# A graph network's attention edges: SyncE's store program as a loop with registers, or written out

## The chip, the cores and the metric

The kernel runs on one core of a Trainium2 chip. What counts is the device time of one execution in microseconds (us). Engines are named as the profile names them: PE is TensorE, DVE is VectorE, ACT is ScalarE, POOL is GpSimd, SP is SyncE. SyncE computes nothing here; it waits for semaphores and issues transfers.

## What is computed

Two graph layers over 12,500 nodes and 200,000 edges, with edges sorted by their destination `dst`. The first layer is a convolution over edges, the second is a pair of attention layers (GAT, four heads of 64 features). The change lies in the attention layers, which the reference writes as:

```python
feat = (h @ W).reshape(n, H, F)
el = jnp.sum(feat * al[None], axis=-1)
er = jnp.sum(feat * ar[None], axis=-1)
e = jax.nn.leaky_relu(el[src] + er[dst], NEG_SLOPE)
m = jax.ops.segment_max(e, dst, num_segments=n)
ex = jnp.exp(e - m[dst])
denom = jax.ops.segment_sum(ex, dst, num_segments=n)
a = ex / denom[dst]
msg = feat[src] * a[:, :, None]
out = jax.ops.segment_sum(msg, dst, num_segments=n)
```

So for each edge a row of `feat` is fetched by `src`, weighted, and the rows of one destination are added up.

## The kernel before

`gat_edges` does the edge part of one attention layer; it runs twice (two stages, with a stage of node work between them). Each of the 128 partitions walks through its own run of 1563 consecutive edges. The run is cut into `SB` = 49 segments of `SBT` = 32 edges. A segment lives in one of `B` = 3 buffers, `gb[:, p]`, with p = s % 3. Five engines work side by side, each with a program of its own, and they meet only at semaphores:

- GpSimd (`rows`, L1821) fetches a segment: 32 indirect transfers, one for each edge place, each of 128 rows. Before a segment `free` waits for three things: the indices `ix` are there (`s_ix`), the stores out of this buffer have landed (`s_st`, segment s-3), and VectorE has finished the first four rows of segment s-2 (`s_sum.at(s, 1, back=2)`).
- VectorE (`body`) starts a segment with L1893 to L1905 (scores, running maximum), waits for ScalarE's exponentials, and then runs a chain of 32 dependent row additions L1927. For each four rows there is one weighting L1915, made one group ahead. The weighting of group k+1 also raises `s_sum`, which tells that group k-1 is done.
- ScalarE makes the exponentials (L1854) and copies the denominators into the rows (L1857).
- SyncE (`body`, L1781 to L1790) stores the finished rows: for each group of four rows a wait for `s_sum` (L1789) and one transfer (L1790) to `sums`; eight of them a segment. Before them it waits until the segment's gathers have landed (L1784), loads the indices of segment s+3 into the same buffer's `ix` (L1779), and waits for ScalarE's copies (`s_seg`, L1788).

On each of these engines the first 45 segments run in a hardware loop `Fori` of 15 rounds, three segments in a round (`LOOPS` = 15). The counter's register gives SyncE the place of a store in DRAM and the values that its waits compare with. What is left is written out behind the loop: segments 45 and 46 in the same `body` with plain numbers, and the last two segments in halves (`ENDS`, function `end`, L1792 to L1796). In `body` a `nop(nofuse=True)` keeps the wait apart from the transfer; in `end` there is none.

PE has no work in these stages.

Of the kernel before, what the change touches and what calls it, by code (L numbers as in the profile page):

```python
# [18 lines left out]
SBT = 32  # L19
SB = -(-E // (SBT * P))  # L20
# [42 lines left out]
def bc(ap, dim, shape):  # L63
    return ap.unsqueeze(dim).to_broadcast(shape)
# [1662 lines left out]
def gat_edges(nc, q, n):  # L1727
# [9 lines left out]
    NQ, B, W = SBT // 4, 3, SBT + 1  # L1737
    LOOPS = (SB - 2) // B
    SPAN = 224
    SPANS = -(-CE // SPAN)  # L1740
    with ExitStack() as c:
# [3 lines left out]
        gb = sb(c, f"gb_g{n}", [P, B, SBT, GR])  # L1745
# [3 lines left out]
        wv = [pb(c, f"wv{k}_{n}", [P, 4, D]) for k in range(2)]  # L1749
        same = sb(c, f"same_g{n}", [P, SBT])  # L1750
        end_masks = [[sb(c, f"end_{y}{x}_{n}", [P, H * (t1 - t0 + 1)], BF16) for y in ("add", "back", "mul")] for x, (_, t0, t1) in enumerate(ENDS)]
        acc = sb(c, f"acc_g{n}", [P, D])

# [3 lines left out]
        s_g = [Signal(q.sem(nm(f"g{p}")), per=SBT, inc=16) for p in range(B)]  # L1757
# [6 lines left out]
        s_st = [Signal(q.sem(nm(f"st{p}")), per=NQ, inc=16, ahead=1) for p in range(B)]  # L1764
        s_dv = q.sem(nm("dv"))
        s_mask = q.sem(nm("mask"))
        out_v = q.sums1.rearrange("(p e) c -> p e c", p=P)
        quads = lambda t0, t1: [slice(t, min(t + 4, t1)) for t in range(t0, t1, 4)]
        summed = lambda x: s_sum.at(SB - 2, 0) + sum(len(quads(t0, t1)) for _, t0, t1 in ENDS[:x])
        line = lambda y, m: y[:, :, :].rearrange("p h t -> p (h t)")[:, 0:H * (m + 1)]  # L1770
        heads = lambda y, m: line(y, m).rearrange("p (h t) -> p h t", h=H)
# [3 lines left out]
        with nc.Block(no_gpsimd_drain=True) as block:  # L1775
            @block.sync
            def _(eng):
                def indices(s, p):
                    eng.dma_start(ix[:, p, :], a["src_chunks"].rearrange("p (s t) -> s p t", t=SBT)[s, :, :]).then_inc(s_ix[p].sem, 16)  # L1779

                def body(s, i, p, more):  # L1781
                    if more:
                        eng.wait_ge(s_g[p].sem, s_g[p].at(i))
                        eng.nop(nofuse=True)  # L1784
                        indices(i * B + (p + B), p)
                    eng.wait_ge(s_seg.sem, s_seg.at(s))
                    for k, ts in enumerate(quads(0, SBT)):
                        eng.wait_ge(s_sum.sem, s_sum.at(s, k + 1))  # L1788
                        eng.nop(nofuse=True)  # L1789
                        eng.dma_start(out_v[:, bass.ds(s * SBT + 4 * k, 4), :], gb[:, p, ts, :]).then_inc(s_st[p].sem, 16)  # L1790

                def end(x, s, t0, t1):  # L1792
                    eng.wait_ge(s_seg.sem, s_seg.at(SB - 2 + x))
                    for k, ts in enumerate(quads(t0, t1)):
                        eng.wait_ge(s_sum.sem, summed(x) + k + 1)
                        eng.dma_start(out_v[:, s * SBT + ts.start:s * SBT + ts.stop, :], gb[:, s % B, ts, :]).then_inc(s_st[s % B].sem, 16)  # L1796

                for s in s_st:
                    eng.sem_inc(s.sem, s.base)
                for p in range(B):  # L1800
                    indices(p, p)
                eng.dma_start(ch, q.er_start[0:EC, :].rearrange("(p e) h -> p (e h)", p=P)).then_inc(s_ch, 16)
                eng.dma_start(q.sums1_x[EC:, 0:D], a[f"L1_gnn_b{n}"].unsqueeze(0).to_broadcast([EP + 1 - EC, D])).then_inc(s_none, 16)
                eng.dma_start(q.sums1_x[EC:EP, D:GR].rearrange("(p r) c -> p r c", p=P), bc(q.unit[:, :], 1, [P, (EP - EC) // P, GR - D])).then_inc(s_none, 16)
                eng.dma_start(q.sums1_x[EP:, D:GR], q.unit[0:1, :]).then_inc(s_none, 16)
                with eng.Fori(0, LOOPS) as i:
                    for p in range(B):
                        body(i * B + p, i, p, True)
                for p in range(B - 1):
                    body(LOOPS * B + p, LOOPS, p, p == 0)  # L1810
                for x, e in enumerate(ENDS):
                    end(x, *e)
                eng.wait_ge(s_st[0].sem, s_st[0].at(SB // B, sum(len(quads(t0, t1)) for s, t0, t1 in ENDS if s == SB - 1)))
                for p in range(1, B):
                    eng.wait_ge(s_st[p].sem, s_st[p].at(SB // B - 1))
                eng.wait_ge(s_none, 48)
# [197 lines left out]
```

## Time and profile before

| what | value |
|---|---|
| time, median of 3 runs | 8455.34 us (8423.16 to 8462.91) |
| the profiled execution's span | 8387.7 us |
| GpSimd busy | 5479.5 us, 65% of the span |
| VectorE busy | 5313.3 us, 63% of the span |
| GpSimd's gathers in the edge stages, L1821 | 3126, 2962.1 us busy, 1567.2 us idle before them |
| VectorE's row additions, L1927 | 3024, 1448.4 us busy, 1278.1 us idle before them |
| SyncE's stores of the edge stages, `sums<-gb_g` | 780 transfers of 528.0 KB, and 2 of 396.0 KB |

The profiled execution is one of its own; its span, from the first to the last instruction, is 67.6 us shorter than the median of the runs. Times within the profile are counted from the start of the span. "Idle before" is the time in which the engine did nothing just ahead of such instructions; it costs something only where the engine is the one that others wait for. In the profile SyncE's instructions are listed as SPq: EVENT_SEMAPHORE is a wait, FUSED_REGOPS, MOVE and ALU_OP work on registers, DMA_DIRECT2D issues a transfer.

### The profile page before, as it was taken

To read this page: it belongs to the slowest core of one execution; us is meant where nothing else is said; L and a number is where in the kernel's file an instruction comes from. 1 tells how busy PE (TensorE), PEld (TensorE's weight loads), DVE (VectorE), ACT (ScalarE), POOL (GpSimd) and SP (SyncE) were. 2 spreads that over 40 slices of the span, in tenths; PEclk is the share of its full clock that TensorE was granted. 3 is DMA by queue.
4 is the path that set the end of the run, shared out by engine and by line. 5 is a ranking of instruction groups with operands and counts; after the bars stand their busy time and mean duration, and the time that the engine had idled before them with its cause. 6 is when DMAs were issued, how large, how long until landed. Compare 5 with 4: busy or idle time off the path is not lost. (4 is left out here: it accounts for less than half of the span.)

```text
span 8387.7 us, 62428 instructions
## 1 busy us (share of the span) xinstructions
PE 2475.3 (30%) x11337; PEld 1696.4 (20%) x11337; DVE 5313.3 (63%) x9727; ACT 2244.0 (27%) x5114; POOL 5479.5 (65%) x5324
## 2 busy tenths in 40 slices
PE   5777677777777485000000000014000000000000
PEld 4444444444444264000000000003000000000000
DVE  6777788877777476465555555653355555565556
ACT  3666677766766352000000000002000000000002
POOL 4777677776777446666666666646666666666664
PEclk8888889988988698555555555557555555555555
DMA  7555555555555457565655555643555555555566
GB/s 236 160 162 163 155 170 169 171 164 160 169 168 164 121 151 204 172 192 184 189 179 187 181 186 181 189 153 93 151 186 185 181 184 184 186 185 187 182 191 219
DMA packets 791709, 1466.03 MB, mean 175 GB/s; under 512 B 188921, under 2 KB 522174, under 8 KB 791100
## 3 DMA queue, kind: packets, MB, share of 16 engines
q0 software_dynamic: 250192, 671.13, 29.9%
q1 hardware_dynamic: 541420, 793.88, 27.1%
q8 instruction: 28, 0.46, 0.0%
q14 instruction: 69, 0.57, 0.0%
HBM read 752.61 MB, written 713.36 MB: 175 GB/s over the span
## 5 line engine op out<-in xcount | busy, mean ns | idle before, releaser
L1821 POOL DMA_INDIRECT gb_g<-table,ix_g x3126 | 2962.1, 948 | 1567.2 <-issue 937.9
L585 POOL DMA_INDIRECT gb<-table,src x1563 | 1890.5, 1210 | 698.2 <-issue 472.9
L1927 DVE SCALAR_TENSOR_TENSOR gb_g<-gb_g,same_g,wv 128x256 f32<-128x256 f32 x3024 | 1448.4, 479 | 1278.1 <-DVE gb_g L1927 554.9
L1096 PE MATMUL pm<-ident,tl 128*4 128x128 f32 x2 | 0.7, 374 | 4655.1 <-DMA tl<-sums 4655.1
L619 PE MATMUL po<-parts,sel 128*128 128x256 f32 x3930 | 1034.6, 414 | 530.7 <-ACT ost L685 347.6
L1854 ACT ACTIVATE ww<-ee 128x132 f32<-128x132 f32 (+3 forms) x102 | 28.5, 280 | 4157.9 <-DVE ee L1905 2160.6
L1915 DVE TENSOR_TENSOR wv<-gb_g,ww 128x1024 f32<-128x1024 f32 x782 | 954.7, 1221 | 0.0
L1096 PEld LDWEIGHTS pm<-ident,tl 128*4 128x4 f32 x2 | 0.2, 81 | 4656.0 <-DMA tl<-sums 4656.0
L619 PEld LDWEIGHTS po<-parts,sel 128*128 128x128 f32 x3930 | 769.5, 204 | 778.4 <-issue 543.4
L762 DVE TENSOR_TENSOR pt<-gb,pt 128x256 f32<-128x256 f32 x392 | 164.6, 420 | 584.5 <-ACT pt L679 451.2
L679 ACT ACTIVATE pt<-pt,sh 128x128 f32<-128x128 f32 x1568 | 436.9, 345 | 344.4 <-remote 200.2
L666 ACT ACTIVATE sq<-iota_f,behind 128x128 f32<-128x128 f32 x1568 | 503.3, 413 | 0.0
L609 PE MATMUL pt<-m,r 64*128 64x256 f32 x3136 | 453.2, 407 | 122.3 <-DVE parts L774 96.8
L685 ACT ACTIVATE ost<-po 128x1024 f32<-128x1024 f32 x393 | 403.2, 1026 | 320.7 <-remote 226.7
L602 PE MATMUL pm<-r,m 128*128 128x512 f32 x784 | 387.7, 618 | 43.6 <-ACT r L661 25.8
L742 DVE TENSOR_TENSOR dots<-gb,sh 128x768 f32<-128x768 f32 x392 | 370.6, 945 | 33.4 <-DMA gb<-table,src 29.7
L729 DVE TENSOR_TENSOR parts<-parts 128x768 f32<-128x768 f32 x393 | 373.7, 951 | 0.0
L766 DVE TENSOR_TENSOR parts<-pt,sh 128x768 f32<-128x768 f32 x392 | 371.3, 947 | 0.0
L769 DVE TENSOR_TENSOR parts<-gb,pt 128x768 f32<-128x768 f32 x392 | 369.9, 944 | 0.0
L609 PEld LDWEIGHTS pt<-m,r 64*128 64x128 f32 x3136 | 285.0, 189 | 401.2 <-issue 386.4
L661 ACT ACTIVATE r<-pm 128x1024 f32<-128x1024 f32 x294 | 301.6, 1026 | 200.1 <-remote 94.0
L774 DVE TENSOR_TENSOR parts<-gb,pt 128x512 f32<-128x512 f32 x392 | 265.2, 677 | 0.0
(302 smaller groups left out, 4182.0 us busy)
## 6 DMA issues: line engine op xcount, KB each, us to landing
sums<-gb_g SPq DMA_DIRECT2D x780, 528.0 KB
sums<-ost SPq DMA_DIRECT2D x393, 512.0 KB
gb_g<-table,ix_g POOLq DMA_INDIRECT x3126
gb<-table,src POOLq DMA_INDIRECT x1563
table<-f SPq DMA_DIRECT2D x48, 520.0 KB
x<-in_x SPq DMA_DIRECT2D x50, 256.0 KB
at<-in_rbf SPq DMA_DIRECT2D x100, 128.0 KB
hT_d<-hT SPq DMA_DIRECT2D x49, 256.0 KB
```

The costliest lines, as they stand in the source:

```text
L585: eng.indirect_dma_start(out=gb[:, group(k), half(k) + j, 0:4, :].rearrange("p a c -> p (a c)"), out_offset=None, in_=q.table0[:, :], in_o ...
L602: ins = eng.matmul(pm[:, g, :], m23[:, n, :], r[n][:, g, :], start=True, stop=True)
L609: ins = eng.matmul(pt[k % 2][:, 2 * h + j, :], r3[hid(h), pair(k), group(k) % 2, j0:j0 + P], m4[hid(h), :], start=True, stop=True)
L619: ins = eng.matmul(po[:, j, :], sel[:, k % 4, j, :], y.rearrange("p a c -> p (a c)"), start=y is parted[0], stop=y is parted[-1])
L666: ins = eng.activation(sq[:, 4 * (k % 2) + j, :], q.iota_f[:, :], ACT.Square, scale=2.0, bias=behind2[:, bass.ds(i * (4 * K) + (4 * (k - 1 ...
L679: ins = eng.activation(w, w, ACT.Copy, scale=sh[:, group(k), 4 * ((k - 1) % 2) + j, 0:1])
L685: eng.activation(ost[:, k % 4, :, :], po[:, :, :], ACT.Copy).then_inc(s_ev.sem, 1)
L729: eng.tensor_tensor(m, m, tmp[:, k % 4, 0:BOTH, :, :], ALU.add).then_inc(s_msg.sem, 1)
L766: eng.tensor_tensor(msg[:, b, :, 1:4, :], bc(w[:, :, 1, :], 2, [P, 4, 3, C]), s1, ALU.mult)
L1821: eng.indirect_dma_start(out=gb[:, p, j, 0:FR], out_offset=None, in_=q.table1[:, :], in_offset=bass.IndirectOffsetOnAxis(ap=ix[:, p, j:j + ...
L1915: return eng.tensor_tensor(wv[k % 2][:, 0:n, :].rearrange("p t (h c) -> p t h c", c=C), f, bc(w, 3, [P, n, H, C]), ALU.mult)
L1927: ins = eng.scalar_tensor_tensor(rows[:, t0 + t, 0:D], row, same[:, t:t + 1], wv[k % 2][:, j, :], ALU.mult, ALU.add)
```

## The change

SyncE's loop in `gat_edges` is replaced by straight code: all 47 whole segments are written out by the Python program, so that each store has its place and each wait its value as a constant. The `nop(nofuse=True)` in front of the transfers is gone, so that a wait may become part of the transfer behind it. The programs of the other four engines keep their loops; number, size and order of the transfers and what each waits for stay as they were. It is made for both attention layers.

```diff
--- before.py
+++ after.py
@@ -1778,16 +1778,14 @@
                 def indices(s, p):
                     eng.dma_start(ix[:, p, :], a["src_chunks"].rearrange("p (s t) -> s p t", t=SBT)[s, :, :]).then_inc(s_ix[p].sem, 16)
 
-                def body(s, i, p, more):
+                def body(s, p, more):
                     if more:
-                        eng.wait_ge(s_g[p].sem, s_g[p].at(i))
-                        eng.nop(nofuse=True)
-                        indices(i * B + (p + B), p)
+                        eng.wait_ge(s_g[p].sem, s_g[p].at(s // B))
+                        indices(s + B, p)
                     eng.wait_ge(s_seg.sem, s_seg.at(s))
                     for k, ts in enumerate(quads(0, SBT)):
                         eng.wait_ge(s_sum.sem, s_sum.at(s, k + 1))
-                        eng.nop(nofuse=True)
-                        eng.dma_start(out_v[:, bass.ds(s * SBT + 4 * k, 4), :], gb[:, p, ts, :]).then_inc(s_st[p].sem, 16)
+                        eng.dma_start(out_v[:, s * SBT + 4 * k:s * SBT + 4 * k + 4, :], gb[:, p, ts, :]).then_inc(s_st[p].sem, 16)
 
                 def end(x, s, t0, t1):
                     eng.wait_ge(s_seg.sem, s_seg.at(SB - 2 + x))
@@ -1803,11 +1801,8 @@
                 eng.dma_start(q.sums1_x[EC:, 0:D], a[f"L1_gnn_b{n}"].unsqueeze(0).to_broadcast([EP + 1 - EC, D])).then_inc(s_none, 16)
                 eng.dma_start(q.sums1_x[EC:EP, D:GR].rearrange("(p r) c -> p r c", p=P), bc(q.unit[:, :], 1, [P, (EP - EC) // P, GR - D])).then_inc(s_none, 16)
                 eng.dma_start(q.sums1_x[EP:, D:GR], q.unit[0:1, :]).then_inc(s_none, 16)
-                with eng.Fori(0, LOOPS) as i:
-                    for p in range(B):
-                        body(i * B + p, i, p, True)
-                for p in range(B - 1):
-                    body(LOOPS * B + p, LOOPS, p, p == 0)
+                for s in range(SB - 2):
+                    body(s, s % B, s + B < SB)
                 for x, e in enumerate(ENDS):
                     end(x, *e)
                 eng.wait_ge(s_st[0].sem, s_st[0].at(SB // B, sum(len(quads(t0, t1)) for s, t0, t1 in ENDS if s == SB - 1)))
```

## Rows read from the trace of the kernel before

**Rows 1.** Windows of the two edge stages: us, busy PE, PEld, DVE, ACT, POOL; clock, DMA.

```profile
3301.00:5594.00 2293.00, 0.00 (x0) 0.00 (x0) 1322.00 (x2480) 61.58 (x167) 1466.80 (x1550) 0.50 0.58 183
5901.00:8225.00 2324.00, 0.00 (x0) 0.00 (x0) 1334.09 (x2524) 43.59 (x153) 1482.86 (x1565) 0.50 0.58 183
```

**Rows 2.** GpSimd's gathers L1821 in the first stage: xcount, min/median/max ns; then idle, times.

```profile
L1821 POOL DMA_INDIRECT gb_g<-table,ix_g x1344: 940/946/1097, 3463.8 to 5405.6; - x192
...
  issue: 402.7, 1322
  DVE wv L1915: 221.1, 17
  DMA sums<-gb_g: 67.4, 5
```

**Rows 3.** VectorE's weighting L1915 in two stretches: first and last start.

```profile
L1915 DVE TENSOR_TENSOR wv<-gb_g,ww x6: 1220/1222/1222, 5045.6 to 5060.9; 128x1024 f32<-128x1024 f32 x6
...
L1915 DVE TENSOR_TENSOR wv<-gb_g,ww x4: 1220/1220/1222, 5085.7 to 5106.7; 128x1024 f32<-128x1024 f32 x4
```

**Rows 4.** SyncE's store line L1790 in two stretches, then over both stages.

```profile
L1790 SPq DMA_DIRECT2D sums<-gb_g x5: 332/333/710, 5050.1 to 5062.4; - x5
...
L1790 SPq DMA_DIRECT2D sums<-gb_g x5: 691/700/709, 5084.6 to 5112.6; - x5
...
L1790 SPq MOVE sums<-gb_g x720: 2/691/1397, 3337.4 to 8085.4; - x180
```

**Rows 5.** GpSimd's timeline, restarts: start, duration, instruction [idle before <-what ended it].

```profile
5047.53 0.94 POOL L1821 DMA_INDIRECT gb_g<-table,ix_g  x1 [13.21 <-DVE wv L1915]
...
5140.55 0.94 POOL L1821 DMA_INDIRECT gb_g<-table,ix_g  x1 [13.05 <-DVE wv L1915]
...
5419.90 0.94 POOL L1821 DMA_INDIRECT gb_g<-table,ix_g  x1 [13.35 <-DVE wv L1915]
...
6179.39 0.94 POOL L1821 DMA_INDIRECT gb_g<-table,ix_g  x1 [13.51 <-DMA sums<-gb_g]
...
6320.83 0.95 POOL L1821 DMA_INDIRECT gb_g<-table,ix_g  x1 [19.70 <-DVE wv L1915]
...
8093.33 0.94 POOL L1821 DMA_INDIRECT gb_g<-table,ix_g  x1 [12.84 <-DVE wv L1915]
```

**Rows 6.** VectorE's timeline, first holes after a restart, in the same columns.

```profile
5076.92 0.48 DVE L1927 SCALAR_TENSOR_TENSOR gb_g<-gb_g,same_g,wv 128x256 f32<-128x256 f32 x1 [0.92 <-DVE gb_g L1927]
...
6221.53 0.48 DVE L1927 SCALAR_TENSOR_TENSOR gb_g<-gb_g,same_g,wv 128x256 f32<-128x256 f32 x1 [0.92 <-DVE gb_g L1927]
...
8139.13 0.48 DVE L1927 SCALAR_TENSOR_TENSOR gb_g<-gb_g,same_g,wv 128x256 f32<-128x256 f32 x1 [0.48 <-DVE gb_g L1927]
```

**Rows 7.** SyncE's stores with constant places, and its loops' branch.

```profile
L1796 SPq DMA_DIRECT2D sums<-gb_g x30: 332/332/432, 5538.8 to 8219.0; - x30
...
L1806 SPq COMPARE_BRANCH  x30: 2/700/712, 3493.8 to 8089.6; - x30
```

**Rows 8.** Written-out ends of both stages: SyncE's waits and stores; VectorE's weighting L1915.

```profile
L1789 SPq EVENT_SEMAPHORE  x15: 17/17/3968, 8090.3 to 8141.9; - x15
...
L1790 SPq DMA_DIRECT2D sums<-gb_g x15: 332/332/394, 8092.6 to 8142.0; - x15
...
L1790 SPq DMA_DIRECT2D sums<-gb_g x6: 332/332/700, 5455.5 to 5491.0; - x6
...
L1915 DVE TENSOR_TENSOR wv<-gb_g,ww x4: 1219/1222/1223, 5457.4 to 5478.4; 128x1024 f32<-128x1024 f32 x4
```

**Rows 9.** VectorE's timeline, a segment's start-up from L1893 to the second L1915, twice.

```profile
5065.96 0.18 DVE L1893 COPY same_g<-samep 128x32 f32 x1 [0.28 <-DVE gb_g L1927]
...
5071.33 1.22 DVE L1915 TENSOR_TENSOR wv<-gb_g,ww 128x1024 f32<-128x1024 f32 x1
...
5119.86 0.18 DVE L1893 COPY same_g<-samep 128x32 f32 x1 [1.79 <-remote]
...
5134.42 1.22 DVE L1915 TENSOR_TENSOR wv<-gb_g,ww 128x1024 f32<-128x1024 f32 x1
```

## The prediction

> **What bounds the kernel now.** First the windows of the two attention edge stages: 2293.0 and 2324.0 us, 4617 of the span's 8387.7 us [rows 1]. The diff touches nothing outside them, so the rest of the kernel is left alone.
>
> Next GpSimd's gathers, since neither it nor VectorE is busy all the time. In the first stage 1344 gathers, 42 segments of 32, run from 3463.8 us to the restart at 5419.90 us: 1956.1 us, 46.57 us a segment. One gather takes 0.946 us and 402.7 / 1322 = 0.305 us lie before the next [rows 2, 5], so an unbroken stream would need 32 x 1.251 = 40.0 us. The other 6.6 us are pauses: 221.1 us in 17 that VectorE's L1915 ends and 67.4 us in 5 that a store's landing ends. GpSimd may gather segment s only when the first four rows of s-2 are summed, so a pause says that VectorE is late.
>
> Why it is late is in the weighting L1915, one for each four rows. In one stretch six stand from 5045.6 to 5060.9 us, 3.06 us apart; in another four stand from 5085.7 to 5106.7 us, 7.0 us apart. One takes 1.22 us in both, so VectorE isn't computing longer, it stands idle [rows 3]. With its start-up of 5.4 or 14.6 us [rows 9] and eight such steps, a segment takes some 30 to 34 us at the quick pace and 70 us at the slow one. GpSimd needs 40.0: only slow stretches cost time.
>
> SyncE has the same two paces. Quick: a transfer holds it for 333 ns. Slow: 700 ns, and the transfers of five stores stand from 5084.6 to 5112.6 us, 7.0 us apart, which is five instructions (wait, two for the place, transfer, counter) at 1.4 us. A register move, which has less to do than a transfer, has a median of 691 ns over the loops: SyncE is in the slow pace for more than half of them [rows 4].
>
> When does it turn? A gather stream restarts at 5047.53 us; VectorE shows its first 0.92 us hole at 5076.92, 29 us later; the next restart is 5140.55, so a cycle of two segments is 93.02 us, 46.5 each. The other kind restarts at 6179.39, has its first hole before 6221.53, 42 us later, and restarts at 6320.83: 141.44 us, three segments ((141.44 - 19.70) / 1.251 = 97, that is 96 gathers and a small rest), 47.1 each [rows 5, 6]. So turning 13 us later was worth nothing: the cycle holds one segment more, and all of its third segment is slow. Of the first layer's 42 segments and 22 pauses, 18 cycles of two and 2 of three make both counts.
>
> **The change part by part.** *What goes.* In the loop a segment costs SyncE 8 stores x 5 instructions and some 6 for the indices and the segment's wait; after it, one transfer that carries its wait, for each store, one more wait for a segment's first store, and one transfer for the indices: about 45 instructions become 10. The kernel has such stores already: 30 at L1796, 332 ns each [rows 7]. Directly this is worth 8 x 4 instructions of an estimated 30 ns (the quick wait is 17 ns [rows 8]), about 1 us a segment of SyncE's time at the quick pace. It lies beside VectorE's 34 to 70 us and takes nothing off the path: a store's landing ended 5 pauses of 22, and the first rows of the next segment follow it by little. Without that cover the most would be those 67.4 us of pauses in each stage.
>
> *The loop's branch* goes too, 30 of them, median 700 ns like any other SyncE instruction and at most 712 [rows 7]; 30 x 0.7 = 21 us of SyncE, hidden in the same way. The Trainium skill ("Runtime: NRT & Kernel Launch", Instruction fetch mechanics) says that a taken branch can cost a fetch of its target while straight code is streamed. By it the unrolling would gain at each branch; the row shows no branch longer than its neighbours, so I count none. About a thousand instructions of straight code more for both layers are fetched; none of the straight stores that exist shows a hole, so that is nothing as well.
>
> *What it may do to the slow stretches* is the only term of size. The kernel of before ends each stage with straight SyncE code of two instructions a store (the loop is over, the rest is written out), which is a trial of half the change. In the second layer the stream restarts at 8093.33 us. From 8092 to 8142 SyncE makes 15 stores, waits at 17 ns median and transfers between 332 and 394 ns: it doesn't turn slow at all. VectorE has its first hole before 8139.13, 46 us after the restart [rows 5, 6, 8]. In the loop SyncE was slow 33 us after a restart [rows 4, 5]. So a light SyncE moves the turn from 29 us, or 42, to about 46. But it doesn't abolish it, and once slow it changes nothing: in the first layer's end SyncE's transfers are at 332 ns and VectorE's L1915 still stands 7.0 us apart, 5457.4 to 5478.4 [rows 8].
>
> What 46 us gives: all cycles become those of three segments. Against 141.44 us the turn is 4 us later; VectorE gains 4 x (1 - 3.06 / 7.0) = 2.3 us, so 139.1 us, 46.4 a segment. If the turn comes still later, past the second segment's end, the third one's start-up runs quick: 5065.96 to 5071.33 is 5.4 us, the slow one 5119.86 to 5134.42 is 14.6 us [rows 9]. That takes off 9.2 us more, 129.9 us, 43.3 a segment. One instruction a store is lighter than the two of the trial, so I go a little past the first value, by its row the nearer: 46.0. Against 46.57 that is 0.57 us on some 94 segments (two layers of 49, less the written-out ends): 54 us.
>
> The bounds: no slow stretch at all, 40.0 us a segment, 94 x 6.6 = 620 us less. On the other side all cycles as the worst seen, 47.1: 94 x 0.55 = 52 us more.
>
> The profiled execution has 8387.7 us of span, the median of the runs is 67.6 us above it; what lies around the span isn't changed. 8387.7 - 54 = 8334, and with those 67.6, 8401 us.
>
> **The rivals.** (a) *Later turn*, as above: 8401 us, 8300 to 8430. For it: no slow SyncE instruction in 49 us of the trial [rows 8]. Against it: one trial, in which VectorE's code was straight too from 8111 us on.
>
> (b) *Nothing*: the turn isn't SyncE's doing, and SyncE is only a second victim of what slows VectorE. For it: with SyncE idle between its stores VectorE stayed at 7.0 us [rows 8]. Cycles stay at two and three segments: 8455 us, 8415 to 8497. The Trainium skill ("Perfetto Trace Analysis", DMA Instruction — HWDGE) says that the block which makes a transfer's descriptors is shared by the VectorE and SyncE sequencers. If that sharing were the hindrance, it would stay, since as many transfers remain, and this case would hold; VectorE slow while SyncE issues one 332 ns transfer in 7 us speaks against that cause [rows 8].
>
> (c) *Slower*: the turn comes at 42 to 46 us in all cycles, just before the second segment ends, where the whole third one is slow. Then all cycles have 47.1 us a segment or a little more: 8455 + 52 = 8507 us, up to 8540. It decides from the point where more than half of the cycles of two become cycles of three without getting shorter. For it: this is just what the five late cycles did; 46.4 of (a) is only 0.7 away.
>
> (d) *The slow stretch mostly gone*: with one instruction the turn comes so late that GpSimd pauses once in five or more segments: 41.5 to 43.3 us a segment, 94 x (3.3 to 5) = 310 to 470 us less, 7985 to 8145 us. Against it: the turn in the trial.
>
> **How the numbers follow.** Chances: (a) 0.42, (b) 0.24, (c) 0.20, (d) 0.14. About 0.5%, 42 us, is what a measurement of this kernel can tell from no change. Of (a) some 0.31 lie below 8413 us; with (d) that is faster 0.45. The rest of (a) and 0.23 of (b) are the same, 0.34. (c) and the edge of (b) are slower, 0.21. The likeliest is (a), 8401 us. Its own range is 8300 to 8430; the range 8 times in 10 leaves out most of (d) and the top of (c): 8180 to 8515.
>
> **What the profile after would show.** SyncE's stores in both stages one line of transfers with a median near 332 ns instead of 691, no register instructions: if they are still at 700 ns, a light SyncE isn't out of the slow pace and (b) holds. GpSimd's pauses: fewer than the 22 and in cycles of three or more segments for (a), the same number for (b). L1915 still 7.0 us apart in the slow stretches, first hole 46 to 52 us after a restart. If the first hole stays at 29 us, the step on the turn is wrong; if it comes at 42 to 46 with cycles of 141 us, it is (c). I am wrong altogether if the time outside the two stages moves, or if the slow pace is tied to VectorE's own loop code.

## The result and the profile after

The changed kernel takes 8387.07 us (median of 5 runs, 8343.07 to 8407.43), the kernel before 8439.66 us (5 runs, 8423.16 to 8462.91) beside it. The ratio is 0.9947, 95% interval 0.9922 to 0.9972: 0.53% faster, or 24 to 66 us. Forecast were 8401 us, 54 less than the 8455 known then; measured are 52.6 less.

The profiled execution of after has a span of 8385.4 us and a time of its own of 8387.07 us. So only 1.7 us lie around a span, and the 67.6 us by which the span of before stood below its median were not launch but a difference between executions (medians of the same kernel on the three chips of the runs below are 8378.5 to 8424.5 us); the forecast carried them along as a constant.

GpSimd's gathers in the first attention layer (layer 1 below), the same 1344 as in [rows 2] (the line numbers behind SyncE's block are 5 lower now: L1816 for L1821, L1910 for L1915, L1922 for L1927). Columns: count, min/median/max ns, first to last start; then idle time before them by what ended it:

```profile
L1816 POOL DMA_INDIRECT gb_g<-table,ix_g x1344: 940/946/1098, 3495.9 to 5412.9; - x192
its engine sat idle before it (us, times) until:
  issue: 402.7, 1322
  DVE wv L1910: 262.5, 21
  DMA sums<-gb_g: 0.3, 1
```

The stream itself is unchanged: 402.7 us of issue in 1322 gaps, to the digit ("issue" is idle time that ended with nothing the profile shows). Stops for VectorE and for stores were 221.1 + 67.4 = 288.5 us and are 262.8: 25.7 us less over 42 segments, 0.61 us each. From the first of these gathers to the restart behind them it was 1956.1 us, and is 5425.91 - 3495.9 = 1930.0, 45.95 us a segment against 46.57.

GpSimd's restarts (start, duration, then idle time and what ended it), and VectorE's first hole in between, as in [rows 5, 6]; the last two lines are layer 1's written-out end:

```profile
5057.37 0.94 POOL L1816 DMA_INDIRECT gb_g<-table,ix_g  x1 [11.95 <-DVE wv L1910]
5087.67 0.48 DVE L1922 SCALAR_TENSOR_TENSOR gb_g<-gb_g,same_g,wv 128x256 f32<-128x256 f32 x1 [0.80 <-DVE gb_g L1922]
5150.06 0.94 POOL L1816 DMA_INDIRECT gb_g<-table,ix_g  x1 [12.80 <-DVE wv L1910]
...
5425.91 0.95 POOL L1816 DMA_INDIRECT gb_g<-table,ix_g  x1 [12.07 <-DVE wv L1910]
5471.16 0.48 DVE L1922 SCALAR_TENSOR_TENSOR gb_g<-gb_g,same_g,wv 128x256 f32<-128x256 f32 x1 [0.92 <-DVE gb_g L1922]
```

The hole comes 30.3 us after a restart in the loops and 45.3 us after it in the written-out end. Over all restarts of both layers (a hole is a pause of more than 0.4 us ahead of a row addition):

| | before | after |
|---|---|---|
| cycles of two segments | 36, mean 92.96 us | 42, mean 91.96 us |
| first hole after the restart | 29.96 us | 31.24 us |
| GpSimd's pause | 13.19 us | 12.15 us |
| cycles of three segments | 5, mean 141.8 us | none in the loops |

SyncE's stores and its waits over both stages, then VectorE's weighting in a quick and a slow stretch, which answer to [rows 4] and [rows 3]:

```profile
L1788 SPq DMA_DIRECT2D sums<-gb_g x752: 319/320/485, 3369.5 to 8157.9; - x188
...
L1787 SPq EVENT_SEMAPHORE  x94: 17/17/17, 3369.4 to 8112.1; - x94
...
L1910 DVE TENSOR_TENSOR wv<-gb_g,ww x5: 1220/1222/1222, 5058.5 to 5070.7; 128x1024 f32<-128x1024 f32 x5
...
L1910 DVE TENSOR_TENSOR wv<-gb_g,ww x4: 1222/1222/1223, 5093.7 to 5114.7; 128x1024 f32<-128x1024 f32 x4
...
L1910 DVE TENSOR_TENSOR wv<-gb_g,ww x8: 1222/1222/1225, 5486.5 to 5534.6; 128x1024 f32<-128x1024 f32 x8
```

SyncE is out of the slow pace for good (320 ns at most 485, where the median of a MOVE was 691). VectorE isn't: four weightings from 5093.7 to 5114.7 us still stand 7.0 us apart. The last row is the last whole segment of layer 1, all of it slow. So the two ends gave back part: from the last gather's start to the last store took 43.4 and 53.2 us before, and takes 70.2 and 69.9. That goes with the segment at which GpSimd's last restart falls: in every profile here in which VectorE turns slow, a restart at segment 48 (counted from 0) leaves an end of 43 to 49 us, at 47 one of 53 to 55, at 46 one of 67 to 71. Before the change they fell at 48 and 47, after it twice at 46, so a part of each total here is where the cycles happen to stop and not their pace. In this pair of executions the two stages, from first gather to last store, went from 2306.5 + 2315.1 to 2295.2 + 2296.6 us, 29.8 less. What lies outside them is unchanged code; it took 3766.1 us before and 3793.6 after, and between 3733.5 and 3806.5 over the profiles of all kernels here. So the spans of this one pair differ by 2.3 us only, and the medians tell the gain.

### The profile page after: what moved, and what is told of

It is laid out like the page before. It is cut to its first block and busy times, and to the rows that moved or that the text cites. A ratio compares the mean times of both kernels' runs of the same rounds, so it can differ in the third digit from the quotient of the medians.

```text
span 8385.4 us, 59216 instructions
## 1 busy us (share of the span) xinstructions
PE 2488.6 (30%) x11337; PEld 1707.7 (20%) x11337; DVE 5316.5 (63%) x9727; ACT 2244.0 (27%) x5114; POOL 5471.9 (65%) x5324
## 5 line engine op out<-in xcount | busy, mean ns | idle before, releaser
L1816 POOL DMA_INDIRECT gb_g<-table,ix_g x3126 | 2963.9, 948 | 1491.8 <-issue 940.1
L1922 DVE SCALAR_TENSOR_TENSOR gb_g<-gb_g,same_g,wv 128x256 f32<-128x256 f32 x3024 | 1449.4, 479 | 1234.3 <-DVE gb_g L1922 537.7
L1910 DVE TENSOR_TENSOR wv<-gb_g,ww 128x1024 f32<-128x1024 f32 x782 | 955.1, 1221 | 0.0
```

The source lines that it names most:

```text
L1816: eng.indirect_dma_start(out=gb[:, p, j, 0:FR], out_offset=None, in_=q.table1[:, :], in_offset=bass.IndirectOffsetOnAxis(ap=ix[:, p, j:j + ...
L1910: return eng.tensor_tensor(wv[k % 2][:, 0:n, :].rearrange("p t (h c) -> p t h c", c=C), f, bc(w, 3, [P, n, H, C]), ALU.mult)
L1922: ins = eng.scalar_tensor_tensor(rows[:, t0 + t, 0:D], row, same[:, t:t + 1], wv[k % 2][:, j, :], ALU.mult, ALU.add)
```

## The experiments

What is to be told apart is what makes VectorE turn slow some 30 us after a restart, and so what SyncE's shorter program changed. **Theory 1**: VectorE's own instructions since the restart, its loop code among them. **Theory 2**: the instructions of all engines, which share something. **Theory 3**: the rate of the gathers alone.

All are timed against the kernel before on the chip on which they ran. In the table, instructions a segment are those of all engines in the trace, averaged over 30 segments; us a segment is from the same 1344 gathers of layer 1 to the restart behind them, over 42.

| run | instructions a segment | us a segment | ratio, 95% interval |
|---|---|---|---|
| before | 147 | 46.57 | 1 |
| the change | 112 | 45.95 | 0.9947 (0.9922 to 0.9972) |
| sync_five | 143 | 46.57 | 1.0011 (0.9991 to 1.0031) |
| pe_four | 144 | 46.52 | 1.0001 (0.9982 to 1.0021) |
| spaced_one | 144 | 46.55 | 1.0008 (0.9991 to 1.0024) |
| nofuse_kept | 119 | 45.48 | 0.9912 (0.9896 to 0.9929) |
| v_straight | 104 | 45.34 | 0.9897 (0.9881 to 0.9914) |
| v_straight_loop | 139 | 46.27 | 1.0005 (0.9989 to 1.0021) |
| half_stores | 108 | 45.75 | 0.9937 (0.9913 to 0.9962) |
| all_straight_half | 96 | 46.48 | 1.0029 (1.0016 to 1.0041) |
| v_straight_spaced_one | 136 | 46.39 | 0.9981 (0.9963 to 1.0000) |
| gather_spaced | 208 | 45.37 | 0.9806 (0.9790 to 0.9821) |
| spaced_two | 176 | 45.10 | 0.9786 (0.9767 to 0.9806) |
| all_straight_half_spaced | 192 | 45.25 | 0.9809 (0.9792 to 0.9826) |

**Is it the register work or the number of instructions? (sync_five)** Straight code, constants, but five instructions a store again:

```diff
                         eng.wait_ge(s_sum.sem, s_sum.at(s, k + 1))
+                        for _ in range(3):
+                            eng.nop(nofuse=True)
+                            eng.wait_ge(s_seg.sem, s_seg.at(s))
+                        eng.nop(nofuse=True)
                         eng.dma_start(out_v[:, s * SBT + 4 * k:s * SBT + 4 * k + 4, :], gb[:, p, ts, :]).then_inc(s_st[p].sem, 16)
```

> The changed kernel, SyncE straight and with constants, but with four waits that are long fulfilled ahead of each store's transfer: five instructions a store as in the loop, no register instruction. Theory 2: the number of SyncE's instructions is what counted, so the hole goes back from 31.2 to 30.0 us and the cycles of two from 91.96 to 92.96 us, a few cycles of three come back, ratio to the kernel before 1.000 (0.998 to 1.003), SyncE's instructions at 0.7 us in the slow stretch. Theory 1 and 3: only the hold of the store's place and counter mattered; hole 31 us, ratio 0.9947.

Measured 1.0011: all of the gain is gone. The gathers of layer 1, and SyncE's stores:

```profile
L1820 POOL DMA_INDIRECT gb_g<-table,ix_g x1344: 942/949/1102, 3453.9 to 5389.4; - x192
its engine sat idle before it (us, times) until:
  issue: 403.0, 1322
  DVE wv L1914: 277.3, 22
...
L1792 SPq DMA_DIRECT2D sums<-gb_g x752: 2/691/1396, 3328.3 to 8170.7; - x188
```

SyncE has its 691 ns again, cycles of two are 92.94 us with the hole at 30.3 us, and two late cycles of 141.9 us are back: the kernel before in all its marks. (The extra waits were three a store and the store's own wait; the text on record says four.) So registers, branch and the place of the store were worth nothing that shows by themselves; it was the instructions as such.

**On an engine that nobody waits for (pe_four).** The same four waits a group, at the same moments, on TensorE:

```diff
+            @block.tensor
+            def _(eng):
+                for s in range(SB - 2):
+                    for k in range(NQ):
+                        eng.wait_ge(s_sum.sem, s_sum.at(s, k + 1))
+                        for _ in range(3):
+                            eng.nop(nofuse=True)
+                            eng.wait_ge(s_seg.sem, s_seg.at(s))
+                        eng.nop(nofuse=True)
```

> The changed kernel, its SyncE as it is, with TensorE, which has no work in these stages, doing four waits for each group of four rows: as many instructions as the run with five a store added on SyncE, and at the same moments, on an engine for which nobody waits. If it is the sum over all engines that counts: the first hole back from 31.2 to about 30.3 us, cycles of two segments from 91.96 to 92.9 us, ratio to the kernel before about 1.000. If it counts only that SyncE itself is slow (its stores late, or its place in what it shares with VectorE): hole 31.2, cycles 91.96 us, ratio 0.9947.

Measured 1.0001, cycles of 93.04 us, hole at 29.4 us. In the trace:

```profile
L1826 POOL DMA_INDIRECT gb_g<-table,ix_g x1344: 940/946/1098, 3494.3 to 5433.6; - x192
its engine sat idle before it (us, times) until:
  issue: 403.0, 1323
  DVE wv L1920: 284.9, 21
...
L1819 PEldq EVENT_SEMAPHORE  x2256: 51/51/51, 3368.0 to 8215.1; - x188
...
L1788 SPq DMA_DIRECT2D sums<-gb_g x752: 319/320/484, 3368.0 to 8214.8; - x188
```

SyncE stays light and quick (320 ns), TensorE's waits take 51 ns each and never more, and VectorE still loses what it had won. So SyncE's lateness isn't the way by which SyncE hurt VectorE. The likeliest reading is that the instructions of all engines use something together; what it is no run shows.

**On GpSimd (spaced_one).** One long fulfilled wait behind each gather:

```diff
                                            in_offset=bass.IndirectOffsetOnAxis(ap=ix[:, p, j:j + 1], axis=0)).then_inc(signal, 16)
+                    eng.wait_ge(s_ini, 16)
+                    eng.nop(nofuse=True)
```

> The changed kernel with one fulfilled wait behind each gather instead of the three of the run above: a gather each 1.251 + 0.054 = 1.305 us (three made 1.414). If VectorE's slow pace needs a stream above some rate between 1.414 and 1.305 us a gather: slow stretches remain, 45 to 46 us a segment, ratio 0.985 to 0.995. If already this stream leaves VectorE quick: 32 x 1.305 = 41.8 us a segment and some pauses, 42 to 44, against 45.98 of the change 190 to 370 us less, ratio 0.95 to 0.972. If GpSimd's own instructions count as SyncE's do: no gain, 0.994 to 1.000.

Measured 1.0008, the third case, with cycles of 92.98 us. The estimate of 1.305 us a gather was wrong: issue is 403.0 us in 1323 gaps as before, a wait is 17 ns and lies within the 0.305 us between gathers. So the run is a third engine's 32 instructions a segment, with the same answer; its semaphore is one that nobody changes in these loops, so signals to the waiting engine aren't needed for the harm.

**Part of the change undone (nofuse_kept).** Straight and constant, the wait apart from the transfer:

```diff
                         eng.wait_ge(s_sum.sem, s_sum.at(s, k + 1))
+                        eng.nop(nofuse=True)
                         eng.dma_start(out_v[:, s * SBT + 4 * k:s * SBT + 4 * k + 4, :], gb[:, p, ts, :]).then_inc(s_st[p].sem, 16)
```

> One part of the change undone: SyncE stays straight with constants, but a store's wait stays apart from its transfer, two instructions a store instead of one. If a segment's time follows the number of all engines' instructions (104 a segment gave 45.40 us, 108 gave 45.70, 112, the change, 45.92, 136 to 147 gave 46.3 to 46.7), 119.5 a segment give 46.0 to 46.2 us, ratio to the kernel before 0.995 to 0.998. If the fused wait itself were the point: 46.4 us, 1.000; if the register work and the loop were: 45.9 us, 0.9947.

Measured 0.9912, below each case: 7 instructions a segment more than the change, and cycles of 90.99 us with the hole at 32.8. So the number of instructions isn't the whole of it, and dropping the `nop` gained nothing. It isn't waits alone that count either: this run keeps the wait of every store and drops the register work, 45 instructions of SyncE a segment becoming 17, and the gain is there. Its interval overlaps the change's (0.9896 to 0.9929 and 0.9922 to 0.9972), and the two were not timed on one chip: whether the fused wait costs something stays open. Sorted by instructions, the runs with VectorE slow look like two levels rather than a line: cycles of 90.7 to 92.0 us from 104 to 119 instructions a segment, 92.7 to 93.0 from 136 to 147. No run lies between 119 and 136, and all_straight_half below, with 96, fits neither.

**VectorE's loop written out (v_straight, v_straight_loop).** The end of layer 1 had its hole at 45 us, with VectorE's code straight too:

```diff
-                with eng.Fori(0, LOOPS) as i:
-                    for p in range(B):
-                        whole(i, p)
-                for p in range(B - 1):
-                    whole(LOOPS, p)
+                for s in range(SB - 2):
+                    whole(s // B, s % B)
```

once on top of the change, and once with SyncE's loop kept.

> The changed kernel with VectorE's loop written out too: 53 instructions a segment instead of 61, the register instructions at a segment's start are gone. Theory 1 (the turn is set by VectorE's own instructions since the restart, as the hole 45 us after the restart in the written-out end of layer 1 says): the first hole comes 42 to 46 us after every restart instead of 31, and the cycles of two segments become cycles of three. At 46.0 to 47.1 us a segment (the late cycles of the kernel before) that is 8387 to 8490 us, ratio to the kernel before 0.994 to 1.006; if the third segment starts quick, 43.3 us a segment, 8135 us, ratio 0.964. Theory 2 (the instructions of all engines count together, and SyncE's 35 fewer a segment moved the hole by 1.2 us): 8 fewer a segment move it by 0.3 us, cycles of two stay at 91.7 us, ratio 0.993. Theory 3 (neither; the gathers alone set it): hole 31 us, ratio 0.9947 as the change.

> The kernel before, SyncE's loop with registers kept, with VectorE's loop alone written out. Theory 1: the same as with SyncE written out, first hole 42 to 46 us after a restart and cycles of three, ratio within 0.5% of that run. Theory 2: hole at 30 to 31 us, cycles near 92.7 us, ratio 0.998. Theory 3: 1.000.

With the change 0.9897: cycles of 90.66 us, hole at 32.5 us, stops of 235.7 us in the 1344 gathers against 262.8. The hole isn't at 42 to 46, so VectorE's loop code doesn't set it by itself (theory 1 falls); the cycles are 1.30 us shorter, where theory 2 gave 0.3. With SyncE's loop kept 1.0005: 38 cycles of two with the hole at 29.7 us, 92.92 us each, and four cycles of three of 139.1 us, three of them with the hole at 45 us and one at 64. So the late turn of theory 1 is there, but in four cycles of 42. VectorE's eight instructions fewer gained something that shows only where SyncE's are gone too, which again looks like two levels and not a sum of independent shares.

**Half as many stores (half_stores).** Eight rows a store:

```diff
-                    for k, ts in enumerate(quads(0, SBT)):
-                        eng.wait_ge(s_sum.sem, s_sum.at(s, k + 1))
-                        eng.dma_start(out_v[:, s * SBT + 4 * k:s * SBT + 4 * k + 4, :], gb[:, p, ts, :]).then_inc(s_st[p].sem, 16)
+                    for k, ts in enumerate(eights(0, SBT)):
+                        eng.wait_ge(s_sum.sem, s_sum.at(s, 2 * k + 2))
+                        eng.dma_start(out_v[:, s * SBT + 8 * k:s * SBT + 8 * k + 8, :], gb[:, p, ts, :]).then_inc(s_st[p].sem, 16)
```

> The changed kernel with stores of eight rows, four a segment instead of eight: four instructions of SyncE and four transfers with their signals less in each segment, the same bytes. If each instruction and each transfer's signal takes a share of what they have in common, the hole moves on by 1 to 2 us and the cycle gets 0.5 to 1 us shorter: ratio 0.990 to 0.993. If only the instructions count and SyncE's are so few already that the rest is in VectorE and GpSimd: 0.994 to 0.995.

(`eights` cuts a segment in eights; the counts of `s_st` and the ends follow.) Measured 0.9937, between its cases and not to be told from the change. Its 38 cycles of two are 91.32 us with the hole at 32.7, which is the first case (0.64 us shorter, 1.4 us later); four cycles of three stand among them, 137.9 us in the mean. In one of these the hole comes late, 55.7 us after the restart:

```profile
7433.28 0.94 POOL L1817 DMA_INDIRECT gb_g<-table,ix_g  x1 [11.99 <-DVE wv L1911]
7489.02 0.48 DVE L1923 SCALAR_TENSOR_TENSOR gb_g<-gb_g,same_g,wv 128x256 f32<-128x256 f32 x1 [0.77 <-remote]
7565.59 0.94 POOL L1817 DMA_INDIRECT gb_g<-table,ix_g  x1 [12.44 <-DVE wv L1911]
```

This cycle takes 132.3 us, 44.1 a segment, where the other three have the hole at 44.6 to 46.6 us and take 138.6 to 140.8.

**All loops written out (all_straight_half).** GpSimd's, ScalarE's and VectorE's loops as SyncE's, and stores of eight rows:

> The changed kernel with the loops of VectorE, GpSimd and ScalarE written out too, and stores of eight rows: an estimated 96 instructions a segment over all engines. By the slope of the runs (0.52 us for the 8 from 112 to 104) it is 44.9 us a segment, about 1.0 us under the change, 94 x 1.0 = 94 us: ratio 0.980 to 0.985. If the gain stops where VectorE's loop code is gone: 45.4 us, 0.988 to 0.990.

Measured 1.0029, slower than the kernel before, with the fewest instructions of all. Two restarts and the hole between them:

```profile
4033.91 0.95 POOL L1817 DMA_INDIRECT gb_g<-table,ix_g  x1 [19.93 <-DVE wv L1905]
4076.08 0.48 DVE L1917 SCALAR_TENSOR_TENSOR gb_g<-gb_g,same_g,wv 128x256 f32<-128x256 f32 x1 [0.91 <-issue]
4174.44 0.95 POOL L1817 DMA_INDIRECT gb_g<-table,ix_g  x1 [19.97 <-DVE wv L1905]
```

Here is the turn of the forecast, 42 us after the restart in this cycle and 46.1 in the mean, with 26 cycles of three segments of 139.0 us, 46.3 a segment, and the pause ahead of a restart at 18.9 us in the mean instead of 12. A turn that moves from 30 to 33 us shortens the cycle of two; one at 42 to 46 us lets GpSimd go on into a third segment, which is then slow throughout. Against v_straight, with its hole at 32.5 us, this run drops the loops of GpSimd (36 to 34 instructions a segment) and ScalarE (5 to 3) and half the stores. Which of them moved the turn isn't shown: the large stores, of which half_stores showed no cost, and the two loops weren't taken out one by one.

**GpSimd held instead (gather_spaced, spaced_two, v_straight_spaced_one, all_straight_half_spaced).** The diff of spaced_one with `for _ in range(3):` and `range(2)` ahead of the wait, on the change; one wait on v_straight; three on all_straight_half.

> The changed kernel with three long fulfilled waits behind each gather on GpSimd, an estimated 3 x 50 ns: a gather each 1.40 us instead of 1.25, 44.8 us a segment of an unbroken stream. Theory 3 (it is the rate of the gathers that drives VectorE and SyncE into the slow pace): the hole comes later by more than the stream is stretched (12%), 36 us or more, or not at all; without a slow stretch 44.8 us a segment, 94 x 1.2 = 113 us less than the change, 8275 us, ratio 0.98. Theories 1 and 2 (instructions of VectorE, or of all engines; GpSimd's are now four a gather): hole at 31 us or earlier, the slow stretch lasts longer, 49 us a segment, 8670 us, ratio 1.027.

> The changed kernel with two fulfilled waits behind each gather. One such wait took the gain away (1.0008), three gave 0.9806 with GpSimd itself stopping for 2 to 4 us between gathers and VectorE quick nearly everywhere. By the number of instructions (176 a segment): cycles of 93 us, VectorE slow, 0.998 to 1.003. If the engine that issues most is held first, GpSimd with three instructions in 1.25 us is held before VectorE with five in 3.06: GpSimd stops between gathers, VectorE stays quick, 0.970 to 0.985.

> The same one wait behind each gather, with VectorE's loop written out beside SyncE's. If the two gains are of one budget, the slow stretch comes later than in either alone: below both, 0.5% or more under the run with the wait alone; if the gather's pace decides alone: the same as that run within 0.3%.

> All loops written out, stores of eight rows, and three fulfilled waits behind each gather. If fewer instructions elsewhere let GpSimd run on longer before it is held: below the three waits alone, 44.5 to 45.2 us a segment, ratio 0.970 to 0.978. If GpSimd is held by its own instructions alone: 45.4 us, 0.978 to 0.982, the same as with the loops.

One wait a gather cost the gain, also with VectorE straight (0.9981, cycles of 92.70 us). By its number that is the second case, 0.27% from spaced_one, though the gathers' pace didn't change; the wait takes back what the straight code gave. Two and three gave 0.9786 and 0.9806, the best of all. Spaced_two's gathers, with what ended the idle time before them:

```profile
L1816 POOL DMA_INDIRECT gb_g<-table,ix_g x1344: 943/949/1146, 3450.4 to 5343.3; - x192
its engine sat idle before it (us, times) until:
  issue: 618.4, 1344
```

The same gathers in order of time, 8 us of them:

```profile
4116.91 0.95 POOL L1816 DMA_INDIRECT gb_g<-table,ix_g  x1 [0.30 <-issue]
4118.66 0.95 POOL L1816 DMA_INDIRECT gb_g<-table,ix_g  x1 [0.80 <-issue]
4121.46 0.95 POOL L1816 DMA_INDIRECT gb_g<-table,ix_g  x1 [1.85 <-issue]
4124.96 0.95 POOL L1816 DMA_INDIRECT gb_g<-table,ix_g  x1 [2.55 <-issue]
4126.38 0.95 POOL L1816 DMA_INDIRECT gb_g<-table,ix_g  x1 [0.47 <-issue]
```

No gather of this layer waits for VectorE any more; GpSimd itself is held (its added waits, 17 ns in the median, take up to 1409), 1.25 us a gather for a while and then 1.75, 2.8, 3.5. VectorE's row additions over both stages in gather_spaced:

```profile
L1925 DVE SCALAR_TENSOR_TENSOR gb_g<-gb_g,same_g,wv 128x256 f32<-128x256 f32 x3024 | 1449.4, 479 | 192.9 <-DVE gb_g L1925 63.8 <-remote 24.7 <-issue 17.4
```

Their idle time is 192.9 us; it was 1234.3 after the change. So with the most instructions of all VectorE is quick, because GpSimd has become the one that is held, in short stops that spread over the segment. The expectation that a slower stream would do it met the number, 0.98, and is wrong in its cause: the median step between gathers is 1.251 us as before, the waits lie in the gap, and the stops come from GpSimd's own slow pace. Theory 2 as a plain sum, by which gather_spaced would have been at 1.027 and spaced_two at 1.000, doesn't hold here. With fewer instructions elsewhere it is the same (0.9809), which fits GpSimd being held by its own. Most of the lead of these runs is at the ends: from the last gather to the last store 16.2 and 15.2 us in gather_spaced, against 70.2 and 69.9 after the change and 67.3 and 68.3 in v_straight. In the steady stretch it is no quicker than v_straight, 45.37 us a segment against 45.34.

## Why the forecast came out, and which step of it failed

**The size was right by luck, on another road.** Forecast were 0.57 us a segment; layer 1 shows 0.62, and over both layers' loops 36 cycles became 1.0 us shorter and five cycles of three at 47.27 us a segment went: 36 + 5 x 3 x (47.27 - 45.98) = 55 us. The ends gave back 25.6 us of it in the profiled executions: from the last restart to the last store it is 365.2 us for six segments now and was 201.6 for three, where three more at 45.98 would be 137.9. That leaves the 29.8 us of this pair.

**The step that failed** is "a light SyncE moves the turn from 29 us, or 42, to about 46", with "all cycles become those of three segments". The turn went from 30.0 to 31.2 us and the cycles of three disappeared. The forecast had named the signs for it: the first hole staying at 29 us, and about as many pauses as the 22 of before: 21 in the 1344 gathers, each at the end of a cycle of two but the first.

**Why the trial misled.** In the written-out end of before [rows 8] not only SyncE's loop was over, VectorE's, GpSimd's and ScalarE's were too. After the change that end shows the same 45.3 us, the loops 31. With every loop written out the forecast's turn and its 139.1 us and 46.4 us a segment appear nearly to the digit (46.1, 139.0, 46.3), and there is no gain: 1.0029. What a still later turn would give was seen right too, but it comes in single cycles only: 44.1 us a segment with the hole at 55.7 us in half_stores. Where the 0.29% more lies its profile doesn't tell: its two stages are 4609.4 us there, 12.2 less than in that of before, with ends of 71.4 and 55.3 us.

**Two readings of rows.** 18 cycles of two and 2 of three make the 42 segments, but they are 20 cycles, and the pauses counted are 22; two of those, 1.7 and 3.8 us, lie within the cycles of three. And SyncE was slow well ahead of the 33 us after a restart from which the forecast counted: at the restart of 5047.53 us its stores hold it for 680 to 711 ns from 5066.4 us on, 19 us after the restart and 10 us before VectorE's hole. So SyncE turns before VectorE does; that didn't make it the one that sets VectorE's turn.

```profile
L1790 SPq DMA_DIRECT2D sums<-gb_g x2: 680/696/711, 5066.4 to 5073.4; - x2
```

**What held.** SyncE's work is worth nothing directly: in pe_four SyncE is as light and quick as in the change, and the time is at 1.0001. The Trainium skill ("Runtime: NRT & Kernel Launch", Instruction fetch mechanics) lets a taken branch cost a fetch where its target lies outside the two pages of code that the engine holds, not at each branch. Nothing of a gain from the missing branches shows in sync_five, which has none in SyncE's loop and is at 1.0011. SyncE's stores are at 320 ns where 332 was said, the pace of L1910 in slow stretches is 7.0 us, and the kernel is bound where the forecast saw it.

**The rivals.** (b) has the kind of cycles right and its reason wrong: SyncE isn't only a victim, since putting its instructions back slows VectorE again (sync_five). The sharing of a descriptor block by VectorE and SyncE, which the Trainium skill names ("Perfetto Trace Analysis", DMA Instruction — HWDGE), isn't the way: four waits on TensorE, with no transfer, do the same harm, and half the transfers change no time that can be told from the change's (0.9937 and 0.9947). (c) is nearly what happens with all loops out, at 46.3 us a segment where it said 47.1. (d), a stretch mostly gone, came with two or three more instructions a gather, at 45.1 us a segment and not at 41.5 to 43.3: GpSimd's stops took the place of VectorE's.

**What stays open**: what the engines' instructions have in common, why the cycles fall into two levels, whether the wait apart from the transfer is really better than the fused one, and what the large stores and the loops of GpSimd and ScalarE each have to do with the 1.0029. A rival that no run here tests is the recording itself: every execution timed here comes with a span and a granted clock, so its instructions were being recorded, and a cost of that would go by their number on all engines too.

## What to carry to other kernels

A trial found inside the old trace is only as good as its list of differences: write down every engine's code in that stretch before one engine gets the credit. Where an engine is late with its instructions no longer than usual, test for a shared cost by putting the same number of instructions on an engine that nobody waits for. And where two engines take turns in being held, removing work moves the turn against a boundary, so less can be slower; holding the producer in many short stops was worth more here (0.9786) than any removal, mostly through shorter ends (33.2 and 29.3 us).

## What was not expected of the hardware

- 32 waits a segment on TensorE, 51 ns each and in no one's way, made VectorE's cycle 1.1 us longer (93.04 against 91.96), just as 31 on SyncE and 32 on GpSimd did (92.94, 92.98).
- Under a stream of gathers it changes who is held: VectorE, and SyncE with five instructions a store, at steps of 0.7 us where GpSimd has one instruction a gather; GpSimd where it has three or four, and then VectorE runs at its quick pace. That the engine which issues most is held fits these runs but for the two with one wait behind each gather: GpSimd has 68 instructions a segment there, and VectorE, with 61 or 53, is still the one held.
- Waits behind a gather were free as far as GpSimd's own pace goes: with one, the gathers still start 1.25 us apart.
